# Attention kernel on one core: the product with V made for two key tiles in a row, in two slots instead of four

## What is computed

```python
x = _ln(src) * (1.0 + scale) + shift
q, k, v = (x @ W + b).reshape(B, S, 16, 32).transpose(0, 2, 1, 3)   # for Wq, Wk, Wv
scores = jnp.einsum('bhqd,bhkd->bhqk', q / math.sqrt(32), k) + attention_bias
probs = jax.nn.softmax(jnp.where(src_mask, -jnp.inf, scores), axis=-1)
ctx = jnp.einsum('bhqk,bhkd->bhqd', probs, v)                       # the product the change moves
x = x + (ctx @ Wo + bo)
h = _ln(x) * g2 + beta2
out = rotate(x + _gelu2(h @ W1 + b1) @ W2 + b2, theta, phi)
```

## Time and profile before

| what | us |
|---|---|
| median of three runs | 3478.37 |
| the profiled execution's own time | 3482.46 |
| its span, first to last instruction | 3480.7 |
| attention stage, from the first product with V to the last transposes | 1595.76 |
| from there to the end (feed-forward) | 1781.04 |
| one batch of attention (batch 8, slot 16 to the same slot of batch 9) | 101.6 |

### The profile page before, as it was taken

The page is one execution under the profiler, slowest core; times in us unless marked ns, Lnnn a source line. Parts: engine busy times, 40 slices in busy tenths (PEclk is TensorE's granted clock), DMA queues, the critical chain, the costliest instruction groups (busy, mean ns, idle before and its releaser), DMA issues. The chain is left out here.

```text
span 3480.7 us, 52432 instructions
## 1 busy us (share of the span) xinstructions
PE 3345.3 (96%) x17104; PEld 2460.4 (71%) x17104; DVE 2022.8 (58%) x4242; ACT 1619.0 (47%) x3493; POOL 2162.8 (62%) x1467
## 2 busy tenths in 40 slices
PE   5999999999999999999769999999999999999998
PEld 4667767677676667767447777777777777777776
DVE  4777777777777777777443444434444434444443
ACT  3777777777777777777422222222222222222221
POOL 3888888788888787887343455544455544555443
PEclk9999999999999999999879999999999999999999
DMA  5988889999898989988520011111011110011100
GB/s 175 271 262 257 263 247 276 257 264 268 250 267 249 265 265 259 263 258 244 181 86 34 16 43 43 43 34 37 16 43 43 37 40 34 19 43 43 37 10 16
DMA packets 288491, 500.87 MB, mean 144 GB/s; under 512 B 43345, under 2 KB 51537, under 8 KB 287729
## 3 DMA queue, kind: packets, MB, share of 16 engines
q1 hardware_dynamic: 288240, 497.60, 48.3%
HBM read 346.39 MB, written 50.40 MB: 114 GB/s over the span
## 5 line engine op out<-in xcount | busy, mean ns | idle before, releaser
L656 POOL TENSOR_TENSOR biasm<-biasm,maskb 128x1024 f32<-128x1024 f32 x512 | 1091.2, 2148 | 264.4 <-DMA biasm<-in_fside_Bx16xSxS_dram 261.5
L1344 POOL TENSOR_TENSOR g_lo<-g,g_hi 128x512 fp32r<-128x512 f32 x256 | 334.8, 1308 | 769.5 <-ACT g_hi L1315 769.5
L1380 DVE SCALAR_TENSOR_TENSOR gate<-ps_h,b_all,gate 128x512 f32<-128x512 f32 x256 | 191.9, 750 | 669.6 <-ACT gate L1305 669.6
L1315 ACT ACTIVATE g_hi<-g 128x512 fp32r<-128x512 f32 x256 | 161.9, 632 | 840.3 <-PE ps_out L1287 444.1
L759 PE MATMUL ps_score<-k_rows,q_rows 96*128 96x512 f32 x1024 | 495.0, 483 | 3.2 <-issue 2.9
L888 DVE CUSTOM_DVE_ANT_0 prob_first<-ps_score,biasm 128x512 f32<-128x512 f32 x512 | 346.9, 687 | 213.2 <-PE ps_score L759 172.2
L1287 PE MATMUL ps_out<-w_hi,g_hi 128*128 128x512 f32 x1024 | 432.0, 422 | 0.0
L888 DVE CUSTOM_DVE_ANT_0 prob_last<-ps_score,biasm 128x512 f32<-128x512 f32 x512 | 346.5, 687 | 120.5 <-PE ps_score L759 109.0
L799 ACT ACTIVATE probT<-ps_probT 128x512 f32<-128x512 f32 x512 | 303.9, 594 | 239.1 <-PE ps_probT L772 236.7
L772 PE MATMUL ps_probT<-ident,prob_first 128*128 128x128 f32 x2048 | 393.0, 273 | 18.6 <-DVE probT L488 14.1
L1257 PE MATMUL ps_h<-h_hi,w_hi 128*128 128x512 f32 x1024 | 406.0, 396 | 3.2 <-issue 1.6
(11 more groups left out here) (142 smaller groups left out, 5945.3 us busy)
## 6 DMA issues: line engine op xcount, KB each, us to landing
biasm<-in_fside_Bx16xSxS_dram SPq DMA_DIRECT2D x512, 512.0 KB, 6.0
k_rows<-k_hi SPq DMA_DIRECT2D x512, 64.0 KB, 5.1
q_rows<-q_hi SPq DMA_DIRECT2D x512, 64.0 KB, 3.5
xn<-in_x_dram SPq DMA_DIRECT2D x16, 1024.0 KB, 7.4
normal_rows<-xn SPq DMA_DIRECT2D x16, 1024.0 KB, 8.4
k_rows<-k_lo SPq DMA_DIRECT2D x256, 64.0 KB, 4.7
q_rows<-q_lo SPq DMA_DIRECT2D x256, 64.0 KB, 4.4
context_t<-rsumT SPq DMA_DIRECT2D x64, 256.0 KB, 5.9
```

Of the source, the lines that this page charges most:

```text
L656: pool.tensor_tensor(tile, tile, maskb[:, 2 * half:2 * half + 2, :], ALU.add).then_inc(masked.sem, 1)
L1344: pool.tensor_tensor(GLO[:, f % 2, :], g[:, :], GHI[:, f % 2, :].bitcast(F32), ALU.subtract)\
L1380: dve.scalar_tensor_tensor(gate[:, :], ps_h[:, f % 2, :], b1_all[:, f:f + 1], gate[:, :], ALU.add, ALU.mult).then_inc(gate_done.sem, 1)
```

## The change

Block `kt` is no longer made in slot i = kt of the first head of a group. In slot i = 0 blocks 0 and 1 are made in a row, in slot i = 2 blocks 2 and 3; slots 1 and 3 have none. The matmuls, their operands, their order and their waits are the same; waits of the second block of a pair now stand right behind the first block, and the score tile, the units and the transposes of slots 1 and 3 stand behind both.

```diff
                     before = group_before(mode, b, g)
-                    if before is not None and h == 0:
+                    for kt in ((i, i + 1) if before is not None and h == 0 and i % 2 == 0 else ()):
                         pb, pg = before
-                        ((outT_act if i % 2 == 0 else outT_dve)
-                         .wait(pe, pb, 2 * (GH * pg + GH - 1) + i // 2))
+                        ((outT_act if kt % 2 == 0 else outT_dve)
+                         .wait(pe, pb, 2 * (GH * pg + GH - 1) + kt // 2))
                         if pg == 0:
-                            v_done.wait(pe, *v_event(pb, i))
-                        if i == 0:
+                            v_done.wait(pe, *v_event(pb, kt))
+                        if kt == 0:
                             ctx_done.wait(pe, b - 1 if g == 0 else b, NG - 1 if g == 0 else g - 1)
                         for hh in range(GH):
                             head = GH * pg + hh
-                            mm = pe.matmul(ps_ctx[HD * hh:HD * (hh + 1), 0, :], V[:, (NT * pb + i) % VR, HD * head:HD * (head + 1)],
-                                           probT[:, hh, i, :], start=(i == 0), stop=(i == NT - 1),
+                            mm = pe.matmul(ps_ctx[HD * hh:HD * (hh + 1), 0, :], V[:, (NT * pb + kt) % VR, HD * head:HD * (head + 1)],
+                                           probT[:, hh, kt, :], start=(kt == 0), stop=(kt == NT - 1),
                                            skip_group_check=True)
                         mm.then_inc(pv_done.sem, 1)
```

## The result

The changed kernel takes 3471.31 us (median of 10 runs, 3466.32 to 3475.48) against 3479.11 us before (10 runs, 3476.55 to 3481.67). The ratio is 0.9977 with a 95% interval of 0.9967 to 0.9987: faster by 0.23%, 7.8 us, where 18.8 had been forecast.

What follows compares the result with a forecast made beforehand. TensorE was taken to set the pace, except in slots 32 to 35, bound by a cross-engine chain. Terms -31.7 + 7.9 + 4 + 1 = -18.8 us against the 3478.37 median gave 3459.6 us, range 3448 to 3474.

Steps and rivals of the forecast that it cites:

- the saving is worn down: Rival: each of 47 ordinary groups loses another 0.1 to 0.3 us at slots 20, 21, 31 or 52; 3464 to 3473; chance 0.19.
- Smaller terms: DVE back in step at slot 2, ACT catching up, little room for transposes of slots 20, 21, 52: 1 us; DMA stalls uncounted.
- pairs in 48 groups: Two pairs a group each save 0.33 us, 0.66 a group: 31.7 us saved in 48 groups.
- slots 32 to 35, 15 batches: All four blocks precede slot 34's transposes, so k4 starts 0.53 us later: 7.9 us lost over 15 batches.
- falls of the clock behind slot 36: About 1.9 us of TensorE idleness halves the clock in 2 or 3 of 15 batches: 4 us lost, bounds 0 and 26.
- slots 20 and 21: Transposes of slots 20, 21 and 52 have little room: 0 to 0.1 us in 31 groups, taken as 1 us.
- V tile in slot 18: Block 3's loads could precede its V tile by at most 0.1 us, hidden under a running wave: costed at nothing.
- TensorE sets the pace; a second block costs 0.86: In slots outside the x chain TensorE is the bound; a block alone costs 1.19 us, a second in a row 0.86.
- The slower rival: Second block's weight loads not hidden in a pair, so it costs 1.13 us: 3488 to 3493; chance 0.03.
- The chain behind slot 34: Slot 34's transposes lead through ACT and DVE to k4 in slot 36; it starts 0.53 us later in 15 batches.
- The waits of the second block cost nothing: A pair's second block finds its `probT` copies already requested; only slot 18's V tile matters, at most 0.1 us, costed at nothing.
- The x stage gains as well: Rival: the chain behind slot 34 has slack, so all 63 groups save 0.66 us: -41.6 us, 3437; chance 0.05.

Runs made afterwards that it cites:

- the fifth experiment: The kernel before with pairs in slots 32 to 35 alone, one block a slot elsewhere: 3487.43 us, ratio 1.0025.
- The first: The changed kernel with one block each in slots 32 to 35, pairs elsewhere: 3461.23 us, ratio 0.9946 against the kernel before.
- The tenth experiment: Changed kernel with single blocks in slots 32 to 35, statistics in slot 53, elsewhere four blocks in each group's first slot, block 3's V copy in slot 15: 3478.34 us.

## Why the prediction was wrong

The direction was right, the size was not: 7.8 us for 18.8. The measured 3471.31 us lies in the range of 3448 to 3474 only because the range was stretched to take in most of the rival in which the saving is worn down. Most steps stand. The step that failed is among the "Smaller terms": "DVE ... waits for the score in slot 2, so it is back in step", with "the transposes of slots 20, 21 and 52 have little room: 0 to 0.1 us in 31 groups, I take 1 us". I worked DVE out for slots 16 to 19 and carried it over to slots 48 to 51. There DVE has one more instruction, the statistics of slot 50, whose cover was the score's delay behind block 3. It costs 0.54 us in 14 batches, 7.5 us of the 11 that are missing, and moving it gave 10 back.

| term | forecast | measured in the profiled execution |
|---|---|---|
| pairs in 48 groups | -31.7 | 0.65 a group, -31.3 |
| slots 32 to 35, 15 batches | +7.9 | 0.54 each, 8.1 |
| falls of the clock behind slot 36 | +4 (2 or 3 of 1.7) | 5 of 1.4, 7 |
| slot 52 | in the next line | 0.54 in 14 batches, 7.5 |
| slots 20 and 21 | +1 | slot 21 0.08 in 16 batches, 1.2 |
| V tile in slot 18 | 0 | 0 in 15 batches, 1.6 in batch 0 |
| slots 37 and 53 of the last batch | 0 | 1.1 |

These make -31.3 + 8.1 + 7 + 7.5 + 1.2 + 1.6 + 1.1 = -4.8 us; the two profiled spans differ by 7.0. Most of the rest is no work of the change: waits for x in slots 43 to 47 took 3.7 us less in this execution than in the one before, and they differ between any two. Against that, the end of attention behind the last score is 0.6 us longer, with the fall at 1682.8 in it, and feed-forward 1.0 longer.

The span that the forecast gives for its 0.60, 3450 to 3467 "(no clock falls and no small losses, to eight falls)", doesn't follow from its own terms: -31.7 + 7.9 gives 3454.6, and with eight falls of 1.7 and the 1 us it is 3469.2.

Point by point:

- *TensorE sets the pace; a second block costs 0.86.* Right to 0.01 us. The slower rival, a seam that isn't hidden, is dead: the loads at 913.87 stand under the first block's second wave. The rule of the Trainium skill that spoke for it ("TensorE: Matmul & The Clock Gate", "The mechanism"), that a load overlaps running matmuls only if it goes to another row group, doesn't hold for these four column strips, which all use the same rows. The Trainium skill's page "TensorEngine Tiling (Array Packing)", section "Key Properties", states that a change of tiling mode drains the engine. No trace here shows the drain itself; the 0.33 us that each pair saves fit it.
- *The chain behind slot 34.* Right in place and size; the fifth experiment isolates it. The first, which leaves that group alone, puts its slots back to their old times and has no falls.
- *The clock.* That the two waits can bring a fall was right, the number of falls was twice mine. It is 3 of the missing 11 us here, and the number varies from execution to execution. In which batches it falls the prediction could not say, and the runs don't either.
- *The waits of the second block cost nothing.* Right but for batch 0, where POOL is late. "At most 0.1 us" was the sign of a wait with no margin, and I had read it in one batch.
- *The saving is worn down.* This rival is what happened, at 3471, but mostly by way of one named instruction in slot 52 instead of a loss spread over all groups. The tenth experiment shows the spread form of it too, once the row of blocks is long enough.
- *The x stage gains as well.* Refuted by the fifth experiment.

## What to carry to other kernels

Putting array-mode changes together is cheap to price: find one place in the trace where the blocks already stand in a row. What it costs is elsewhere: every instruction that the moved block had covered. So walk each engine's own program through every copy of the pattern, not through one, and list what stands in it only there; here one statistics instruction and one transpose chain took half of the gain, 7.5 + 8.1 of 31.3 us.

Here block 3, in slot 35 behind the start of a long cross-engine chain, was covered by it; moved ahead of it, it turned a gain of 0.66 us a group into a loss of 0.54; and a wait that one moves away may only lead to the next one of the same chain (slot 36 to slot 39).

## What the hardware showed that I had not expected

TensorE's granted clock fell to 1.2 GHz for 3.41 us after waits of 1.86 us in total with transposes and a score between them, and in only 3 to 7 of 15 batches with the same waits to 0.01 us. In batch 15 of the kernel before, 1.65 us were followed by none. In both kernels TensorE waits there 0.32 us ahead of its last score and 1.31 us behind it, and in the changed one the clock did fall right after, at 1682.8. So the length of the waits alone doesn't say whether it falls.

A fall behind slot 36 costs 1.4 us, under the half of 3.41. Of the difference 0.16 us are a wait of slot 39 that shrinks by as much; the rest is not taken apart.
